# SyncE reads its indices as one record a step, and the weight chunk's place once in eight steps

## The reference, cut to what matters

```python
Wi_b, Wo_b = Wi[expert_idx], Wo[expert_idx]          # expert_idx = itok_B_0_7
h = gelu(einsum('bsh,bhi->bsi', x, Wi_b) + bi_b)     # 256 -> 1024
o = einsum('bsi,bih->bsh', h, Wo_b) + bo_b           # 1024 -> 256
x1 = layernorm(o + x) * g_b + be_b
hidden = gelu(einsum('bsd,ad->bsa', x1, down_W) + down_b)
hidden = einsum('bsa,boa->bso', hidden, expert_W[idx]) + expert_b[idx] + domain_emb[idx]
out = layernorm(einsum('bsa,da->bsd', hidden, up_W) + up_b + x1) * ln_gamma + ln_beta
```

## Time and profile before

| | |
|---|---|
| median of 3 runs | 537.85 us (537.72 to 538.39) |
| the profiled execution's own time | 537.86 us |
| its span, first to last instruction | 535.9 us |
| mean granted clock of TensorE | 0.983 |
| PE busy | 493.2 us, 92% of the span |
| PEld / DVE / ACT / POOL busy | 81% / 79% / 71% / 59% |
| DMA: share of 16 engines on the main queue | 31.5% |

### The profile page before, as it was taken

The page is one execution under the profiler, slowest core; times in us unless marked ns, Lnnn a source line. Parts: engine busy times, 40 slices in busy tenths (PEclk is TensorE's granted clock), DMA queues, the critical chain, the costliest instruction groups (busy, mean ns, idle before and its releaser), DMA issues.

```text
span 535.9 us, 19427 instructions
## 1 busy us (share of the span) xinstructions
PE 493.2 (92%) x5778; PEld 432.0 (81%) x5779; DVE 423.7 (79%) x935; ACT 381.8 (71%) x1099; POOL 315.0 (59%) x521
## 2 busy tenths in 40 slices
PE   5699999999999999999989999999999999999962
PEld 3489988888888878888878888888878888888951
DVE  6677888888888888788888888887888877677762
ACT  2688777787877777777778777787777876677741
POOL 5043666666656566565665566655666655555554
PEclk9799999999999999999999999999999999999995
DMA  4734333333333333323333333333333222222111
GB/s 115 245 95 103 87 91 94 79 91 89 93 93 80 87 92 89 92 78 90 91 90 91 84 91 87 90 90 87 87 88 89 63 64 58 61 62 56 46 32 29
DMA packets 70256, 45.83 MB, mean 86 GB/s; under 512 B 43969, under 2 KB 61778, under 8 KB 70098
## 3 DMA queue, kind: packets, MB, share of 16 engines
q1 hardware_dynamic: 69200, 45.25, 31.5%
q10 hardware_dynamic: 1026, 0.21, 0.2%
HBM read 36.51 MB, written 8.91 MB: 85 GB/s over the span
## 4 chain that ended last, share of the span: by engine, by line
SPq 37%; PE 35%; issue 11%; DVE 6%; POOL 4%; DMA 3%; ACT 2%; POOLq 1%; DVEq 0%; ACTq 0%
SPq L258 9%; SPq L322 8%; SPq L372 7%; SPq L330 7%; PE p_h L918 5%; PE p_h L919 4%; PE p_h L920 4%; PE p_o L928 4%; PE p_o L926 4%; PE p_o L927 4%; SPq L338 3%; PE p_d L937 2%; DMA x_T<-in_xT 2%; POOL rs L484 2%; PE p_t L959 2%
## 5 line engine op out<-in xcount | busy, mean ns | idle before, releaser
L918 PE MATMUL p_h<-x_hi,W 128*128 128x128 f16 x1088 | 194.0, 220 | 5.6 <-issue 5.3
L919 PE MATMUL p_h<-x_lo,W 128*128 128x128 f16 x1088 | 193.4, 220 | 0.0
L920 PE MATMUL p_h<-x_hi,W 128*128 128x128 f16 x1088 | 193.3, 220 | 0.0
L484 POOL TENSOR_TENSOR rs<-mv,neg_half 128x2 f32<-128x2 f32 (+1 forms) x70 | 67.6, 966 | 162.4 <-DVE mv L797 156.8
L581 ACT ACTIVATE h<-p_h,bi_tile 128x128 f32<-128x128 f32 x544 | 152.6, 362 | 0.4 <-PE p_h L920 0.4
L926 PE MATMUL p_o<-W,h_hi 128*128 x544 | 148.3, 273 | 0.0
L927 PE MATMUL p_o<-W,h_hi 128*128 x544 | 148.3, 273 | 0.0
L928 PE MATMUL p_o<-W,h_lo 128*128 x544 | 148.3, 273 | 0.0
L764 DVE SCALAR_TENSOR_TENSOR h_lo<-h,h_hi 128x512 f16<-128x512 f32 x136 | 124.5, 915 | 1.0 <-ACT h_hi L589 0.9
L918 PEld LDWEIGHTS p_h<-x_hi,W 128*128 x1088 | 106.7, 98 | 19.7 <-issue 18.3
L919 PEld LDWEIGHTS p_h<-x_lo,W 128*128 x1088 | 106.7, 98 | 1.5
(11 more groups left out here) (153 smaller groups left out, 715.7 us busy)
## 6 DMA issues: line engine op xcount, KB each, us to landing
stage<-in_w SPq DMA_DIRECT2D x56, 256.0 KB, 2.6
x_nat<-in_x SPq DMA_DIRECT2D x136, 64.0 KB, 2.1
out<-y SPq DMA_DIRECT2D x136, 64.0 KB, 2.0
x_T<-in_xT SPq DMA_DIRECT2D x134, 64.0 KB, 2.2
W<-in_w SPq DMA_DIRECT2D x8, 256.0 KB, 4.1
g_t<-in_gamma SPq DMA_DIRECT2D x1, 1024.0 KB, 7.7
W<-in_expert_W SPq DMA_DIRECT2D x2, 128.0 KB, 3.0
upT<-in_up_W SPq DMA_DIRECT2D x2, 64.0 KB, 2.6
```

Of the source, the lines that this page charges most:

```text
L484: pool.tensor_tensor(rs[:, both], mv[:, both, 1], neg_half[:, both], ALU.pow).then_inc(rs_done, 1)
L918: mm(p_h[parity][:, c, :], hi, x_hi[:, parity, k, :], start=(k == 0), stop=False)
L919: mm(p_h[parity][:, c, :], hi, x_lo[:, parity, k, :], start=False, stop=False)
L920: ins = mm(p_h[parity][:, c, :], lo, x_hi[:, parity, k, :], start=False, stop=(k == KD - 1))
```

## The change

The indices of SP are laid out anew. For each step there is now a record of six numbers: the two source indices of tile i, the two of tile i+2, and the two output indices of tile i-5. SP reads a record with one TENSOR_LOAD at the step's start, and the read behind the wait for `y_done` is gone. The record begins at 6i where the old read of six began at 2i. Since the eight chunks of an expert lie one behind the other, only the first one's place is kept, eight numbers instead of 64; SP reads it once in eight steps and adds the chunk's number in the DMA's own address arithmetic. Its loop body now holds eight steps written out, as it must for that. The sorting writes the records: the source indices with two copies in place of one, with a semaphore count of its own for the first, for which ACT waits. The area before PE's records and before the experts has another length, so that these begin at other places in `idx` (PE's at number 438, before 409; POOL's at 730 + i, before 272 + i).

```diff
-IDX_SRC, IDX_DST = 0, SLOTS
-IDX_EXP = 2 * SLOTS + 3
+IDX_SP = 0
+IDX_PE = IDX_SP + 6 * STEPS
+IDX_EXP = IDX_PE + 4 * STEPS + 3
 IDX_CHUNK = IDX_EXP + TILES + 2
-IDX_PE = IDX_CHUNK + CHUNKS
-IDX_LEN = IDX_PE + 4 * STEPS
+IDX_LEN = IDX_CHUNK + E0
...
-            def load_later(j, slot_n):
+            def load_later(j, expert, m, slot_n):
                 if not isinstance(j, int) or j >= SLOTS_W:
                     sp.wait_ge(w_lo, j - (SLOTS_W - 1))
-                c = index(sp, IDX_CHUNK + FIRST_CHUNKS + j, CHUNKS - 1)
-                sp.dma_start(stage[:, slot_n, :], t["w"][bass.ds(c * P, P), :]).then_inc(w_in[slot_n], 16)
+                sp.dma_start(stage[:, slot_n, :], t["w"][bass.ds((expert + m) * P, P), :]).then_inc(w_in[slot_n], 16)
+            def first_chunk(place_n):
+                return index(sp, IDX_CHUNK + place_n, CHUNKS - NCH)
...
-            chunks = indices(sp, IDX_CHUNK, FIRST_CHUNKS // 2, CHUNKS - 1)
-            load_first([chunks[m] for m in FIRST_ORDER[:4]], FIRST_ORDER[:4])
-            load_first(indices(sp, IDX_CHUNK + FIRST_CHUNKS // 2, FIRST_CHUNKS // 2, CHUNKS - 1), FIRST_ORDER[4:])
+            expert = first_chunk(0)
+            for m in FIRST_ORDER:
+                sp.dma_start(first_stage[m], t["w"][bass.ds((expert + m) * P, P), :]).then_inc(first_in[m], 16)
...
             def step(i, parity, four, weights):
                 if weights:
-                    load_later(i + AHEAD, weights[2])
-                if exists(i):
-                    b = indices(sp, 2 * i + IDX_SRC, 6 if exists(i + 2) else 2, B - 1)
+                    if weights[0] == 0:
+                        expert[0] = first_chunk(weights[1])
+                    load_later(i + AHEAD, expert[0], weights[0], weights[2])
+                if exists(i + 2) or exists(i - 5):
+                    b = indices(sp, 6 * i + IDX_SP, 6, SLOTS - 1)
                 if exists(i + 2):
-                    load_turned(b[4:6], i + 2, parity)
+                    load_turned(inside(b[2:4]), i + 2, parity)
                 if exists(i - 5):
                     sp.wait_ge(y_done, i - 4)
-                    to = indices(sp, 2 * i + (IDX_DST - 10), 2, SLOTS - 1)
                     for n in range(2):
-                        sp.dma_start(t["out"][bass.ds(to[n] * S, S), :], y[S * n:S * n + S, 1 - parity, :])\
+                        sp.dma_start(t["out"][bass.ds(b[4 + n] * S, S), :], y[S * n:S * n + S, 1 - parity, :])\
...
-            run(sp, step, SLOTS_W, AHEAD)
+            run(sp, step, NCH, AHEAD)
...
-            act.wait_ge(idx_ready, SRC_READY)
-            b = indices(act, IDX_SRC, 2, B - 1)
+            act.wait_ge(idx_ready, FIRST_READY)
+            b = indices(act, IDX_SP, 2, B - 1)
...
-            v.scalar_tensor_tensor(idx[:, IDX_CHUNK:IDX_PE].rearrange("a (e c) -> a e c", c=NCH), wide(ord_f[:, :]),
-                                   float(NCH), rows(iota_e[0:1, :], E0), ALU.mult, ALU.add).then_inc(idx_ready, 1)
+            v.tensor_scalar(idx[:, IDX_CHUNK:IDX_LEN], ord_f[:, :], float(NCH), None, ALU.mult).then_inc(idx_ready, 1)
...
-            v.tensor_copy(idx[:, IDX_SRC:IDX_DST], p_t[0:1, 0:SLOTS]).then_inc(idx_ready, 1)
+            v.tensor_copy(sp_idx[:, 0:TILES, 0:2], src).then_inc(idx_ready, 1)
+            v.tensor_copy(sp_idx[:, 0:TILES - 2, 2:4], src[:, 2:TILES, :]).then_inc(idx_ready, 1)
```

More of the change, by code:

```diff
@@ L176, in build @@
         y_out = [sem(f"y_out{n}") for n in range(2)]
-        CHUNK_READY, SRC_READY, TILE_READY, ALL_READY = 1, 2, 3, 4
+        CHUNK_READY, FIRST_READY, SRC_READY, TILE_READY, ALL_READY = 1, 2, 3, 4, 5
         iota_ready = sem("iota_ready")
@@ L316, in _, with inside @@
                 sp.dma_start(downb[half, :], t["down_b"].rearrange("(p a) -> p a", a=1)).then_inc(adapter_in, 16)
+            def inside(b):
+                return [nc.s_assert_within(r, 0, B - 1, skip_runtime_bounds_check_because="the sorting clips every index")
+                        for r in b]
             def load_turned(b, i, parity):
@@ L331, in load_natural @@
                       .then_inc(xnat_in[parity], 16)
-            def load_later(j, slot_n):
+            def load_later(j, expert, m, slot_n):
                 if not isinstance(j, int) or j >= SLOTS_W:
                     sp.wait_ge(w_lo, j - (SLOTS_W - 1))
-                c = index(sp, IDX_CHUNK + FIRST_CHUNKS + j, CHUNKS - 1)
-                sp.dma_start(stage[:, slot_n, :], t["w"][bass.ds(c * P, P), :]).then_inc(w_in[slot_n], 16)
+                sp.dma_start(stage[:, slot_n, :], t["w"][bass.ds((expert + m) * P, P), :]).then_inc(w_in[slot_n], 16)
+            def first_chunk(place_n):
+                return index(sp, IDX_CHUNK + place_n, CHUNKS - NCH)
             sp.wait_ge(idx_ready, CHUNK_READY)
-            def load_first(chunks, of):
-                for c, m in zip(chunks, of):
-                    sp.dma_start(first_stage[m], t["w"][bass.ds(c * P, P), :]).then_inc(first_in[m], 16)
-            chunks = indices(sp, IDX_CHUNK, FIRST_CHUNKS // 2, CHUNKS - 1)
-            load_first([chunks[m] for m in FIRST_ORDER[:4]], FIRST_ORDER[:4])
-            load_first(indices(sp, IDX_CHUNK + FIRST_CHUNKS // 2, FIRST_CHUNKS // 2, CHUNKS - 1), FIRST_ORDER[4:])
+            expert = first_chunk(0)
+            for m in FIRST_ORDER:
+                sp.dma_start(first_stage[m], t["w"][bass.ds((expert + m) * P, P), :]).then_inc(first_in[m], 16)
             sp.wait_ge(idx_ready, SRC_READY)
-            b = [indices(sp, 2 * i + IDX_SRC, 2, B - 1) for i in range(2)]
-            load_turned(b[1], 1, 1)
+            load_turned(indices(sp, IDX_SP + 6, 2, B - 1), 1, 1)
+            expert = [first_chunk(1)]
             for j in range(AHEAD):
-                load_later(j, j % SLOTS_W)
+                load_later(j, expert[0], j, j % SLOTS_W)
             sp.dma_start(g_t[:, :], t["gamma"].partition_broadcast(P)).then_inc(g_in, 16)
@@ L361, in step @@
                 if weights:
-                    load_later(i + AHEAD, weights[2])
-                if exists(i):
-                    b = indices(sp, 2 * i + IDX_SRC, 6 if exists(i + 2) else 2, B - 1)
+                    if weights[0] == 0:
[3 more added lines that the diff above has]
+                    b = indices(sp, 6 * i + IDX_SP, 6, SLOTS - 1)
                 if exists(i + 2):
-                    load_turned(b[4:6], i + 2, parity)
+                    load_turned(inside(b[2:4]), i + 2, parity)
                 if exists(i - 5):
                     sp.wait_ge(y_done, i - 4)
-                    to = indices(sp, 2 * i + (IDX_DST - 10), 2, SLOTS - 1)
                     for n in range(2):
-                        sp.dma_start(t["out"][bass.ds(to[n] * S, S), :], y[S * n:S * n + S, 1 - parity, :])\
+                        sp.dma_start(t["out"][bass.ds(b[4 + n] * S, S), :], y[S * n:S * n + S, 1 - parity, :])\
                           .then_inc(y_out[1 - parity], 16)
                 if exists(i):
-                    load_natural(b[0:2], i, parity)
-            run(sp, step, SLOTS_W, AHEAD)
+                    load_natural(inside(b[0:2]), i, parity)
+            run(sp, step, NCH, AHEAD)
             for n in range(2):
@@ L697, in _ @@
             dve.wait_ge(src_row, 1)
-            v.tensor_copy(idx[:, IDX_SRC:IDX_DST], p_t[0:1, 0:SLOTS]).then_inc(idx_ready, 1)
+            sp_idx = idx[:, IDX_SP:IDX_PE].rearrange("a (t r) -> a t r", r=6)
+            src = p_t[0:1, 0:SLOTS].rearrange("a (t n) -> a t n", n=2)
+            v.tensor_copy(sp_idx[:, 0:TILES, 0:2], src).then_inc(idx_ready, 1)
+            v.tensor_copy(sp_idx[:, 0:TILES - 2, 2:4], src[:, 2:TILES, :]).then_inc(idx_ready, 1)
             iota_d = rows(iota_g[:, 0:ENTRIES], PARTS)
@@ L707, in _ @@
             dve.wait_ge(tile_rows, 1)
-            pe_idx = idx[:, IDX_PE:IDX_LEN].rearrange("a (t r) -> a t r", r=4)
+            pe_idx = idx[:, IDX_PE:IDX_PE + 4 * STEPS].rearrange("a (t r) -> a t r", r=4)
             v.tensor_copy(pe_idx[:, 4:TILES + 4, 2:4], p_d[0:1, 0:SLOTS].rearrange("a (t n) -> a t n", n=2))\
@@ L756, in _ @@
             link(v.scalar_tensor_tensor(row, row, float(B), empty, ALU.add, ALU.mult))
-            v.tensor_tensor(idx[:, IDX_DST:2 * SLOTS], row, p_u[0:1, 2 * SLOTS:3 * SLOTS], ALU.add)\
+            v.tensor_tensor(sp_idx[:, 5:TILES + 5, 4:6], row.rearrange("a (t n) -> a t n", n=2),
+                            p_u[0:1, 2 * SLOTS:3 * SLOTS].rearrange("a (t n) -> a t n", n=2), ALU.add)\
                 .then_inc(idx_ready, 1)
```

## The result

The changed kernel takes 525.06 us (median of 4 runs, 524.43 to 525.15), the kernel before 538.06 in the same comparison. The ratio is 0.9756, with a 95% interval of 0.9739 to 0.9773. The forecast was 526.8 us, a gain of 11.1 us from SP's queue leaving the path; the medians differ by 13.0.

What follows compares the result with a forecast made beforehand. SP's queue, 7.40 us a step, was taken to set the pace of the 40 steps from 133.5 to 428.6 us. These fall from 295.1 to 284.0 us: 537.9 - 11.1 = 526.8 us, range 521.5 to 530.3.

Steps and rivals of the forecast that it cites:

- 0.97 us a step less, to 6.43: SP's queue: fewer index reads, register operations and loop branches cut its step from 7.40 to 6.43 us.
- the ring: Chain of each step's work through PE, ACT, DVE and POOL, next to no slack: 7.10 us a step.
- The floor is 28.4 us for four steps: With SP off the path, the 40 steps from 16 to 56 take 284.0 us, not 295.1: 11.1 us less.
- the early piece: Four steps from 105.1 to 133.5 us in the kernel before, taken as the pace without SP's lateness: 28.4 us.
- the long step: Once in four steps PE stands 0.76 us at its loop's branch; about 0.6 us goes into that step.
- the 0.17 us of an ordinary step's start: PE's idle time at a step's start, what a shorter read of PE's record could win; read left at 1.00 us.
- Start 0, between +0.3 and -1.0: Run's start: sorting's extra copy +0.2 us, smaller table under 0.1 less, SP's earlier loads 0.2 less; sum 0.
- Before that stretch SP's lateness costs nothing: Ahead of the 40 steps that begin at 133.5 us, late SP loads cost 0 us, so no gain there.
- A: Rival: PE's branch fits into slack, every step lasts 6.95 us, 520.8 us; 13% with what lies towards the forecast.
- B: Rival: another wait, such as SP's for POOL's `y`, leaves 28.7 us for four steps, 529.8 us; 19%.
- C: Rival: SP's longer loop body stalls at its branch; 10 us a pass would give 551 us; 3%.
- D: Rival: the merged read costs about 1 us more, SP stays at 7.4 us a step, 538 us; 3%.

Runs made afterwards that it cites:

- curve of six kernels: SP's own time a step against the 40 steps' time, six kernels: 6.1 to 7.1 us gives 283.5 to 284.0, 7.4 gives 295.1, 7.5 gives 298.7.
- the second half alone: Kernel before with only the chunk's place read once in eight steps and SP's loop body of eight steps, old reads kept: 525.41 us, ratio 0.9761.
- the second pair: Changed kernel and kernel before, both unaltered, in another execution: 524.83 and 538.13 us; PE's clock rose at about 25.6 and 25.9 us.
- the first pair: Changed kernel and kernel before as first profiled, 525.06 and 538.06 us; PE's clock rose at about 23.9 and 25.8 us.

## Why the prediction was right, point by point

- *SP's queue is the bound.* Right. The curve of six kernels and the wait of ACT that vanished show it.
- *0.97 us a step less, to 6.43.* Right: the step less SP's waits leaves 6.4. One small term was missing: with the sum in its address the issue of the chunk's load takes 0.42 us in place of 0.36. With it the second half alone comes to 7.07 and not to the expected 7.0, just at the ring's pace, and its SP hardly waits.
- *The floor is 28.4 us for four steps.* Right, 28.38. This term, 11.1 us, was measured as 11.3 and 11.7 (two pairs of executions). The pattern is another one: four steps go by 6.95, 6.97, 6.4 and 8.0 us now, in the early piece by 7.54, 6.95, 6.98 and 6.93. That is POOL's moved records, for which the forecast had 0, and as a loan they do cost 0.
- *What makes the long step.* Only half right. I put PE's 0.76 us down to its loop's branch. With the read at 0.33 us the branch costs nothing that can be seen; it took branch and 1.00 us read together to stall PE.
- *PE's read: what could be won is "the 0.17 us of an ordinary step's start", with DVE's own stream right behind.* Wrong, though the forecast doesn't rest on it. The change itself left the read at 1.00 us, as said, but the edit was worth 12 us. For the ordinary step it holds: DVE's stream left 0.04 us to win there. I had not looked at the branch, nor at the run's end.
- *Start 0, between +0.3 and -1.0.* The second copy did hold DVE by some 0.2 us, and PE's next product began 0.07 us later in all. The 0.9 us at step 2 were the clock's.
- *"Before that stretch SP's lateness costs nothing."* Not quite, and this is a part of what the forecast lacked. In the second pair, where the clocks agree, the span is 12.5 us shorter: 0.2 up to step 8, 0.8 from step 8 to 16, 11.7 in the 40 steps, and -0.2 behind them. (In the first pair steps 8 to 16 take 57.1 and 56.1 us.) Some 0.5 us of these eight steps is the loan of one short step, which is paid back behind step 56. The rest is likely SP's lateness: in these steps ACT waited for `x_T` 1.6 and 3.9 us in the two executions before, and not at all in the changed kernel. It was not tried apart, and the kernel with the place read once, whose ACT doesn't wait there either, still takes 56.8 us.
- *Rivals.* A (520.8 us) did not come: the long step stayed. B (529.8) did not: SP waits for `y`, and nobody waits for SP. C did not: at the branch of SP's body of eight steps register operations follow within 0.3 us, as they did before. The Trainium skill's rule ("Runtime: NRT & Kernel Launch", "Instruction fetch mechanics"), by which a body within 512 instructions isn't fetched anew, agrees; no run here had a longer body on SP. D did not: two kinds of read are left on SP, of one index and of six.

The version to use is the one with PE's records at a multiple of four: 513.4 us.

## What to carry to other kernels

An engine that computes nothing has no busy share, and can still set the pace; the sign is a load that is late while its issuing queue never waits. In these kernels such a queue counted only while it was slower than the others, so find that corner before adding savings: half of the edit gave all of the gain. And when a bound goes, price again what was worthless before; beginning PE's records at a multiple of four was worth nothing in the 40 steps before the change and 7 us in them after it.

## What the runs showed of the hardware

How long a read of four or more indices from SBUF into registers takes depends on where it begins. On SP one index took 0.28 us and two 0.47, wherever they began; six took 1.28 when they did not begin at a multiple of four numbers, and 0.73 when they did. On PE four took 1.00 and 0.33 us, on POOL five took 1.17 and 0.56. Away from a multiple of four each further index, from one to six, adds about 0.2 us. That agrees with the Trainium skill, which gives about 200 ns a register ("Runtime: NRT & Kernel Launch", "Instruction fetch mechanics"), there for loads that it says come from HBM; the four in 0.33 us do not agree. Its floor of about 600 ns for such a load ("DMA: Bandwidth & Descriptors", "Latency and other measured facts") doesn't hold here: 0.28 us.

PE's loop branch and its read of 1.00 us stalled PE by 0.68 us together. The read alone, at the start of an ordinary step, left 0.17 us or so, and the branch with a read of 0.33 us nothing.

DVE's L735, the same operation, took 1.21 us while POOL was working on its 128x256 products and 0.68 where POOL was late with them. Moving POOL's short read, so that POOL was in time in every step, made the short ones disappear; that it is POOL's products which stretch L735 was seen in the order of time only.
